# Deformable convolution by table and gather: one table transfer for four row pairs instead of one for each

## The reference, cut to what matters

```
offset = conv2d(x, offset_w, offset_b)              # 18 channels: dy, dx of nine taps
mask   = 2 * sigmoid(conv2d(x, mod_w, mod_b))       # 9 channels
val    = for each tap k and pixel: the bilinear mean of x at (y + ky - 1 + dy, x + kx - 1 + dx), times mask
y      = einsum('bckhw,ock->bohw', val, reg_w)
```

## Time and profile before

| | |
|---|---|
| median of 3 runs | 3220.82 us (3220.05 to 3222.2) |
| profiled execution | 3215.99 us |
| its span, first to last instruction | 3214.2 us |
| mean granted TensorE clock | 0.709 |
| busy in the span | PE 1549.9, DVE 1985.6, ACT 854.6, POOL 1777.7 us |
| table transfers | 768 on SP: 256 of 144.0 KB, 512 of 72.0 KB |

### The profile page before, as it was taken

One profiled execution on the slowest core, in us unless ns is written; L12 is line 12 of the kernel. 1 busy time (PEld: TensorE's weight loads), 2 busy tenths in 40 slices (PEclk: granted clock), 3 DMA queues, 4 the chain that ended last, 5 costly groups with the idle time before them and its releaser, 6 DMA issues. The chain is left out here.

```text
span 3214.2 us, 31625 instructions
## 1 busy us (share of the span) xinstructions
PE 1549.9 (48%) x11604; PEld 893.3 (28%) x11604; DVE 1985.6 (62%) x1764; ACT 854.6 (27%) x1110; POOL 1777.7 (55%) x1353
## 2 busy tenths in 40 slices
PE   3665551222222222222222220263888888888897
PEld 3454420000100001000110000151454555555555
DVE  4222235555545455555555555575999999999995
ACT  2111151111111111111111100154454454444441
POOL 2000027777777777777777777334544544545542
PEclk8778765555555555555555555586999999999999
DMA  9999863655445554555445553313122212212212
GB/s 371 406 429 429 362 161 118 160 154 142 133 135 150 148 136 132 136 151 147 135 131 138 153 144 104 130 31 95 57 66 92 91 65 93 90 65 100 83 63 92
DMA packets 337893, 483.66 MB, mean 150 GB/s; under 512 B 186016, under 2 KB 277940, under 8 KB 320048
## 3 DMA queue, kind: packets, MB, share of 16 engines
q1 hardware_dynamic: 279120, 330.24, 30.3%
q0 software_dynamic: 58720, 152.72, 16.7%
HBM read 397.28 MB, written 85.45 MB: 150 GB/s over the span
## 5 line engine op out<-in xcount | busy, mean ns | idle before, releaser
L438 POOL DMA_INDIRECT gath<-table,idx x1152 | 1217.0, 1056 | 430.5 <-issue 368.3
L613 DVE TENSOR_TENSOR gath<-gath,p_stat 128x2304 f32<-128x2304 f32 x128 | 327.0, 2554 | 745.9 <-DMA gath<-table,idx 643.5
L650 PE MATMUL p_z<-wz,pairs 128*128 128x384 f32 x384 | 262.2, 814 | 450.6 <-issue 447.3
L496 ACT ACTIVATE zt<-p_z 128x384 f32<-128x384 f32 x192 | 93.4, 492 | 981.2 <-remote 604.7
L650 PEld LDWEIGHTS p_z<-wz,pairs 128*128 128x128 f32 x384 | 98.8, 296 | 602.6 <-issue 591.2
L1269 PE MATMUL p_state<-xt,tri 128*128 128x512 f32 x512 | 239.4, 611 | 41.0 <-DVE prod L1158 40.9
L640 PE MATMUL p_conv<-sides,wconv 128*128 128x512 f32 x64 | 66.3, 1139 | 398.0 <-issue 236.1
L1049 POOL TENSOR_TENSOR gated<-gated,outw 128x512 f32<-128x512 f32 x64 | 124.2, 1946 | 210.0 <-ACT gated L1102 210.0
L1158 DVE TENSOR_TENSOR prod<-p_state,query 128x2048 f32<-128x2048 f32 x80 | 182.2, 2277 | 54.1 <-PE p_state L1274 51.5
L1035 POOL TENSOR_TENSOR query<-query,expo 128x2048 f32<-128x2048 f32 x16 | 72.5, 4534 | 254.3 <-DVE expo L1131 254.3
L658 PE MATMUL p_y<-ident,yt 128*128 128x128 f32 x64 | 17.8, 433 | 389.6 <-DVE yt L621 389.6
(11 more groups left out here) (232 smaller groups left out, 3161.2 us busy)
## 6 DMA issues: line engine op xcount, KB each, us to landing
ring<-in_w SPq DMA_DIRECT2D x64, 2304.0 KB, 19.3
hidw<-in_hidw SPq DMA_DIRECT2D x64, 1024.0 KB, 5.2
table<-zt SPq DMA_DIRECT2D x256, 144.0 KB
table<-zt SPq DMA_DIRECT2D x512, 72.0 KB
gath<-table,idx POOLq DMA_INDIRECT x1152
xt<-in_x SPq DMA_DIRECT2D x4, 1024.0 KB, 8.0
resid<-xt SPq DMA_DIRECT2D x32, 128.0 KB, 2.3
xlate<-resid SPq DMA_DIRECT2D x16, 256.0 KB, 2.8
```

The source lines that it names most:

```text
L438: nc.gpsimd.indirect_dma_start(out=gath[:, t % SLOTS, k].rearrange("p n c -> p (n c)"), out_offset=None, in_=tables[u], in_offset=bass.Ind ...
L613: tt(g, g, w, ALU.mult).then_inc(weighted, 1)
L650: nc.tensor.matmul(p_z[i % ZS][:], pairs[u][:, 4 * J:4 * J + 4].rearrange("p j w -> p (j w)"), wz[:, m * WIDE:(m + 1) * WIDE], start=True, ...
```

## The change

The lines of all taps and rows are put in one sequence, so that row y of tap k is line 9·y + 2·k of 34 cells. Rows y and y+2 then follow each other without a break in steps of two lines (9 taps of row y, 9 of row y+2, and so on), and the rows of the other parity fill the gaps. A transfer can so take four row pairs and nine taps: 36 lines by 32 cells. The row pairs are dealt out anew, pair 4r+J to partition block r of group J, so that one block of `zt` holds four neighbouring pairs. SP waits once for all 12 chunks and issues 12 transfers, four of 36×32 whole cells and eight of 36×32 half cells. Ahead of it `pairs` is written and read through a strided view; the coordinates use another multiplier and another offset for each tap. The table has 9 lines that no pixel uses; POOL fills them with zeros too, with two more transfers for each table.

```diff
-    CELLS = WP * WP
+LINES = TAPS * (WP + 1)
-    grid = [t[0:TAPS * CELLS].rearrange("(k y x) c -> k y x c", y=WP, x=WP) for t in tables]
+    lines = [t[0:LINES * WP].rearrange("(s x) c -> s x c", x=WP) for t in tables]
...
                 for e in (0, H, H + 1):
-                    pool.dma_start(grid[u][:, e].rearrange("k x c -> x k c"), blank).then_inc(border_out, 16)
+                    pool.dma_start(lines[u][TAPS * e:TAPS * (e + 2) - 1:2].rearrange("k x c -> x k c"), blank[0:WP]).then_inc(border_out, 16)
+                for first, last in ((1, TAPS), (TAPS * WP, LINES)):
+                    unused = lines[u][first:last:2].rearrange("s x c -> x s c")
+                    pool.dma_start(unused, blank[0:WP, 0:(last - first + 1) // 2]).then_inc(border_out, 16)
...
                 for e in (0, WP - 1):
-                    pool.dma_start(grid[u][:, :, e].rearrange("k y c -> y k c"), blank).then_inc(border_out, 16)
+                    pool.dma_start(lines[u][:, e].rearrange("(y k) c -> y k c", k=TAPS), blank).then_inc(border_out, 16)
...
-    PIECES = RH * 3
+    JOIN = 4
+    PIECES = RH * 3 // JOIN
...
+        def rows_of(u):
+            return pairs[u][:].rearrange("p (j r) w -> p r j w", j=JS)
...
-                for J in range(JS):
-                    sp.wait_ge(z_taken, b * (JS * CHUNKS) + CHUNKS * (J + 1))
+                for J in range(0, JS, JOIN):
+                    sp.wait_ge(z_taken, b * (JS * CHUNKS) + CHUNKS * (J + JOIN))
                     for r in range(4):
-                        y0 = 1 + 2 * (4 * J + r)
-                        mine = zt[u][r * W:(r + 1) * W, J]
-                        column = grid[u][:, :, 1:1 + W].rearrange("k y x c -> y x k c")
-                        sp.dma_start(column[y0], mine.rearrange("x k q c -> x k (q c)")).then_inc(table_out[u], 16)
-                        sp.dma_start(column[y0 + 1][:, :, 0:C], mine[:, :, 1]).then_inc(table_out[u], 16)
-                        sp.dma_start(column[y0 - 1][:, :, C:2 * C], mine[:, :, 0]).then_inc(table_out[u], 16)
+                        mine = zt[u][r * W:(r + 1) * W, J:J + JOIN].rearrange("x j k q c -> x (j k) q c")
+
+                        def column(y):
+                            return lines[u][TAPS * y:TAPS * (y + 2 * JOIN) - 1:2, 1:1 + W].rearrange("s x c -> x s c")
+
+                        y0 = 1 + 2 * (4 * r + J)
+                        sp.dma_start(column(y0), mine.rearrange("x s q c -> x s (q c)")).then_inc(table_out[u], 16)
+                        sp.dma_start(column(y0 + 1)[:, :, 0:C], mine[:, :, 1]).then_inc(table_out[u], 16)
+                        sp.dma_start(column(y0 - 1)[:, :, C:2 * C], mine[:, :, 0]).then_inc(table_out[u], 16)
...
-                        nc.scalar.activation(pairs[u][q * C:(q + 1) * C, js], src[:, q], ACT.Identity, **affine).then_inc(pad_ready, 1)
+                        nc.scalar.activation(rows_of(u)[q * C:(q + 1) * C, 2 * h:2 * h + 2], src[:, q].rearrange("p (r j) w -> p r j w", j=JS), ACT.Identity, **affine).then_inc(pad_ready, 1)
...
-                step(nc.vector.scalar_tensor_tensor(out=flat[:], in0=low[:, :, 0::2], scalar=float(WP), in1=low[:, :, 1::2],
+                step(nc.vector.scalar_tensor_tensor(out=flat[:], in0=low[:, :, 0::2], scalar=float(TAPS * WP), in1=low[:, :, 1::2],
...
-                    last = nc.tensor.matmul(p_conv[:, q], wconv[part, 1], pairs[u][part].rearrange("p j w -> p (j w)"), start=False, stop=True)
+                    last = nc.tensor.matmul(p_conv[:, q], wconv[part, 1], rows_of(u)[part], start=False, stop=True)
...
-    a["place_of"] = np.tile((k * (WP * WP) + WP + 1).astype(np.float32), (P, NT, 1))
+    a["place_of"] = np.tile((k * (2 * WP) + TAPS * WP + 1).astype(np.float32), (P, NT, 1))
```

More of the change, by code:

```diff
@@ L111, in layer0 @@
         gn = stat_buffers(nc, ctx, "gn0")
-        zero = sb("zero0", [WP, 2 * C])
+        zero = sb("zero0", [WP + 1, 2 * C])
         xh = sb("xh", [P, RH + 2, WP, B])
@@ L153, in _ @@
             pool.wait_ge(zero_ready, 1)
-            blank = zero[:].rearrange("e (o c) -> e o c", o=1).to_broadcast([WP, TAPS, 2 * C])
+            blank = zero[:].rearrange("e (o c) -> e o c", o=1).to_broadcast([WP + 1, TAPS, 2 * C])
             for u in range(2):
                 for e in (0, H, H + 1):
-                    pool.dma_start(grid[u][:, e].rearrange("k x c -> x k c"), blank).then_inc(border_out, 16)
-                pool.dma_start(tables[u][TAPS * CELLS:TAPS * CELLS + 1], zero[0:1]).then_inc(border_out, 16)
-            pool.wait_ge(border_out, 128)
+                    pool.dma_start(lines[u][TAPS * e:TAPS * (e + 2) - 1:2].rearrange("k x c -> x k c"), blank[0:WP]).then_inc(border_out, 16)
+                for first, last in ((1, TAPS), (TAPS * WP, LINES)):
+                    unused = lines[u][first:last:2].rearrange("s x c -> x s c")
+                    pool.dma_start(unused, blank[0:WP, 0:(last - first + 1) // 2]).then_inc(border_out, 16)
+                pool.dma_start(tables[u][LINES * WP:LINES * WP + 1], zero[0:1]).then_inc(border_out, 16)
+            pool.wait_ge(border_out, 192)
             for u in range(2):
                 for e in (0, WP - 1):
-                    pool.dma_start(grid[u][:, :, e].rearrange("k y c -> y k c"), blank).then_inc(border_out, 16)
-            pool.wait_ge(border_out, 192)
+                    pool.dma_start(lines[u][:, e].rearrange("(y k) c -> y k c", k=TAPS), blank).then_inc(border_out, 16)
+            pool.wait_ge(border_out, 256)
         @block.scalar
@@ L649, in multiply @@
                         pe.wait_ge(z_taken, b * (JS * CHUNKS) + (i + 1 - ZS))
-                    nc.tensor.matmul(p_z[i % ZS][:], pairs[u][:, 4 * J:4 * J + 4].rearrange("p j w -> p (j w)"),
+                    nc.tensor.matmul(p_z[i % ZS][:], pairs[u][:, 4 * J:4 * J + 4].rearrange("p r w -> p (r w)"),
                                      wz[:, m * WIDE:(m + 1) * WIDE], start=True, stop=True).then_inc(z_done, 1)
@@ L1363, in build_program @@
         gs = {name: whole.enter_context(nc.semaphore(f"norm_{name}")) for name in STAT_SEMS}
-        tables = [nc.dram_tensor(f"table{u}", (TAPS * WP * WP + 1, 2 * C), F32, kind="Internal").ap() for u in range(2)]
+        tables = [nc.dram_tensor(f"table{u}", (LINES * WP + 1, 2 * C), F32, kind="Internal").ap() for u in range(2)]
         layer0(nc, xt, d, row_stats, tables, gs)
```

## The result

The median after the change is 3231.08 us (3223.43 to 3234.04, 16 runs) against 3222.47 before (3219.27 to 3229.49, 16 runs): ratio 1.0024, interval 1.0017 to 1.0031. It is slower, by 8.6 us or a quarter of a percent. The forecast was +48. The profiled execution took 3232.49, its span 3230.7.

The account below looks back on a forecast made before the run. POOL's gathers were taken as the bound, with late tables making POOL wait: 3216 + 43 (loop) + 4 (batch 0) + 1 (layer 0) = 3264, or 3269 us with the runs' median 4.8 above the profile; range 3190 to 3330.

Parts of the forecast that it names:

- The bound: Second stage's loop: POOL's gathers set the pace, 78.06 us busy and 23.0 idle making a batch of 101.1 us.
- Late table, POOL waits: Loop batches: POOL waits 3 to 7 us for the table; period 104.1 against 100.8, +43 us over 13 periods.
- rival 2: Loop: writes under 25 us, so the table is not late; 3226 down to 3210 us; chance 0.14.
- D: Loop: end of one batch's gathers to first gather of the batch after next, through copies and writes; 108.2 us.
- The copies' term: ACT's `p_z` copies in the loop: 4.9 us apart with SP idle, 53.9 us, upper bound 61.6.
- The run of gathers: POOL's 72 gathers of a loop batch: 100.0 us after the change, 100.5 before.
- list of signs: Loop trace: waits, copy spacing, issues, DMA share and period show right or wrong; gather mean leaving 1.03 to 1.08 means wrong.
- The range: Whole kernel: 3190 to 3330 us; the forecast's own range was 3243 to 3325.
- Batch 0: First gather of batch 0: later table since writes start after all copies; +4 us, between +3 and +7.
- Layer 0 and small edits: Extra border lines in layer 0 cost +1 us, between 0 and 3; strided `pairs` and coordinates cost nothing.
- Rival 1: Loop: many issues slow copies and issues; with 12, copies take some 7 us, time 3121; chance 0.14 in full or part.
- Rival 3: SP's issues in the loop: price per piece, 5.6 us each, 67.2 for twelve; 3508 us; chance 0.06.

Follow-up runs that it names:

- f4: Kernel before with 64 instead of 72 gathers a batch from batch 1 on; 2958.57 us, ratio 0.9521.
- g1: Kernel before, POOL's first gather of a batch held until DVE has weighed the last slot of the batch before; 3184.86 us, ratio 1.0256.
- e2: Kernel before, POOL's first gather of a batch held until DVE has summed the last slot of the batch before; 3226.47 us, ratio 1.0381.
- e8: Kernel before, unaltered, run again for a trace at the short pace; 3106.47 us.
- set 3: Runs at the long pace: kernel before (3218.62 us), idle ACT copies in three kernels, and the changed kernel with batch 0 written as 48 early transfers.
- e7: Kernel before, its 48 transfers held until all 12 chunks are copied; 3117.17 us, ratio 1.0020.
- e12: Changed kernel with batch 0 alone written as 48 early transfers; 3220.58 us, ratio 1.0010.
- e1: Changed kernel with JOIN = 1: new line order, still 48 early transfers a batch; 3107.73 us, ratio 1.0000.
- e6: Changed kernel, unaltered, run at the short pace against the kernel before; 3125.06 us, ratio 1.0041.
- e9: Changed kernel with an idle ACT copy ahead of each loop `p_z` copy but a batch's first; 3228.95 us, ratio 1.0033.
- sets 3 and 5: Two sets of runs on the same chip; the kernel before took 3218.62 us in the first and 3107.86 us in the second.
- e11: Changed kernel with two row pairs a transfer (JOIN = 2) and idle ACT copies in the loop; 3221.54 us, ratio 1.0008.
- e5: Changed kernel, loop writes sent to spare tables and POOL waiting for none of them; 3118.74 us, ratio 1.0024.
- f2: Changed kernel, loop writes sent to spare tables without waits, run once more; 3122.04 us, ratio 1.0036.
- e3: Kernel before, from batch 2 on one transfer a batch to a spare tensor in place of 48; 3104.74 us, ratio 0.9990.

## Why the prediction was right or wrong

- **The bound.** POOL as pacemaker: confirmed at the short pace (f4, g1, e2). At the long pace the kernel after has POOL standing still 75 us longer over eleven batches, and the period moves by 0.3 us. So some 8 us a batch of what the gathers cost in the kernel before wasn't work that POOL had to do; the short intervals between gathers, 697 of 781 after, are as many as in e8 at the short pace.
- **Late table, POOL waits.** Right at the long pace: waits of 7.4 to 9.3 us (forecast 3 to 7), in the earlier trace rows none. At the short pace the table is never late after batch 0, since the copies take 8 us: rival 2's outcome, from another cause.
- **D**, from the end of one batch's gathers to the first gather of the batch after next. Forecast 108.2, measured 110.0 for batches 5 to 7: 16.6 from the gathers' end at 1049.76 to the first copy at 1066.35 (forecast 18.1), copies 61.0 (53.9), 0.5 to the first issue (0.6), writes and landing 31.9 (35.6). The copies' term was wrong: 4.9 apart with SP silent was read from two intervals, and the pace stayed 5.6. The writes' error offset half of it.
- **The run of gathers: the step that failed.** The forecast left it at 100.0 us. It was 92.5 in batch 5, 92.1 to 93.5 from batch 4 on. Two periods are one run and one D, so a run of 100.0 with the measured D would have made the period 105.0; with 92.5 it is 101.3. Those 7.5 us a run, 3.75 a period, are some 49 us over 13 periods, more than the whole error of the forecast. That run and D add up to two periods is arithmetic. What bears the forecast out is that D stayed between 108.5 and 110.6 from batch 4 on, so that late batches did make the next ones late. The forecast had tied the cost of a gather to the writes (batch 15's 99.6), though that row had no write in it and was hardly cheaper, and it had no term for a pause that changes it. Its own list of signs named this one: a mean that leaves 1.03 to 1.08. What makes the gathers of the kernel after cheap stays open; the pause is the likeliest (set 3).
- **The range.** Its upper end was added up with two runs: a D of 115.9 and the 100.0 of the forecast make a period of 108.0 and not 108.2, which takes 3 us off the 3325. It changes nothing in the reading.
- **Batch 0.** Forecast +4; from first copy to first gather 30.5 before and 38.7 after, +8.2. 33.5 us at a share of 0.89 was the row of a batch whose writes run beside gathers; alone, twelve transfers reached 0.69. This term, not the loop, is most of the change's loss: e7 has it with 48 transfers, e12 takes it back.
- **Layer 0 and small edits.** Forecast +1; e1 shows nothing (±3 us). What is left at the short pace, some 6 of e6's 15 us, isn't explained. Only five runs stand behind the 15 (3115.3 to 3125.7), the profiled pair has 8.9, and the first copy alone lies between 424.7 and 431.0 from trace to trace.
- **Rival 1** (many issues make the pace) is refuted from both sides: after and e9 have 12 issues and copies 5.6 apart, e8 has 48 and copies 0.7 apart. **Rival 3**: the issue did grow, to 3.8 us, but twelve took 23.5 us and the engines at 0.87 set the end.
- **Open.** What the long pace is, and why POOL's gathers without a pause then stretch to 1.40 us apart in the mean (72 of them 100.8 us). Whether it is chance that 92.5 us of gathers and a pause of 8.4 come to nearly the same is open too. Shown: the long pace isn't the kernel's (all kernels of a set share it), nor one chip's (sets 3 and 5). The number of transfers (e11, 24 of them) and their order in the table (e1, at the short pace only) are argued against, not excluded. e5 and f2, which take the waits away and leave the 12 transfers, would have settled it at the long pace; both met the short one. No kernel that does the whole work beat the one before: e1 and e12 lie within 0.1%, and so does e3, which leaves writes out.

## What to carry to other kernels

Ask whether the bound's own price per instruction is a cost or only a pace: if the mean far exceeds the usual duration (1056 against a median of 949 here), some of it may be waiting, and a new wait may be paid from it. It is so at one pace and not at the other: a pause of some 8 us a batch was nearly free at the long pace and cost its full length at the short one. Joining transfers of 72 and 144 KB saved nothing here and gave up the overlap with their producers; look first at the batch that nothing covers, where it costs at once. And put the kernel before beside every run: its time moved by 3.6% between sets, fifteen times the effect.

## What the runs showed of the hardware

The same kernel ran at 3107.9 and at 3218.6 us on one chip in two sets. A copy of `p_z` takes 0.49 us at either pace, and the median gather 0.95. But at the long pace twelve copies take some 60 us, not 8, from batch 3 on. The first of them wait with their products ready, and their idle time is booked mostly to `remote`; SP's issues stand 1.40 apart, not some 0.6; a gather costs 1.08 in the mean, not 0.98, where POOL doesn't pause, because nearly half of them last longer. ACT's and SP's intervals come in steps of 0.70 us (copies 4.2, 4.9, 5.6, 6.3, 7.0; issues 0.70, 1.40); POOL's don't (1.25 for more than half). A transfer of 1152 pieces takes 0.3 and 0.6 us to issue for the first two of a batch and up to 3.8 for later ones; at the short pace one of 288 pieces takes 0.52 to 0.57 in the median (e8).
